# Expert weights in DRAM as pieces of 128 partitions x 4 KB, in a two-layer attention and expert kernel

## The chip, the cores and the metric

The kernel runs on one core of one Trainium2 chip. The metric is the device time of one execution in microseconds (us).

## The reference

The input x has 8 sequences of 100 tokens of width 1024 (800 tokens, float32); each sequence also has a context of 722 rows of width 256. Four blocks follow one another, each as x = x + f(layernorm(x)): cross-attention, a mixture of experts, a second cross-attention, and a feed-forward layer with ternary weights. The change touches the mixture of experts alone:

```
logits = h @ gate_w.T + gate_b                  # 32 experts
topk_logits, topk_idx = top_k(logits, 4);  w = softmax(topk_logits)
gate = h @ w_gate[e] + b_gate[e];  up = h @ w_up[e] + b_up[e]     # 1024 -> 512
act  = (clip(up, -7, 7) + 1) * min(gate, 7) * sigmoid(1.702 * min(gate, 7))
y    = sum over the 4 experts of w * (act @ w_down[e] + b_down[e])  # 512 -> 1024
```

## The kernel before

The expert stage (in the profile from about 1389 to 2240 us) works in blocks of 64 token slots of one expert. 800 tokens x 4 experts, each expert rounded up to whole blocks, are split into three queues of equal length; step s takes block s // 3 of queue s % 3, and each queue has a weight buffer of its own in SBUF (`W2`, NQ_W = 3 buffers of 12,288 floats per partition). The first 8,192 floats of a buffer are the gate and up weights (W2_D = KC x 2 x FI, with KC = 8 chunks of the input width and FI = 512), the other 4,096 the down weights (IC = 4 chunks of D = 1024). In both parts a chunk is 1024 floats, which is 4 KB per partition.

An expert's weights are loaded when its queue reaches it, in order of the first step that needs them: 34 loads, because two experts lie across the border of two queues. Each load is a gate-up DMA of 4 MB (L1372, in the loop L1417), two bias DMAs of 128 KB (L1376, L1420) and a down DMA of 2 MB (L1380, in the loop L1424). All of them are issued by SP, in one queue (q1), in program order. In the loop, SP first waits until the gate-up and bias DMAs of the load before have landed and until TensorE has done the last gate-up that used the buffer; the down DMA waits in the same way for the down DMA before it and for the last down product (L1411 to L1424).

A step on TensorE is: half of the gate-up product (L1518), the transposes of the next tile's tokens (L1510) and of the activations of the step before (L1526), the other half of gate-up, and the down product of the step before (L1542). Gate-up waits for weights and biases (`m_wg`), down for its weights (`m_wd`). VectorE adds the bias (L1607, once a step) and computes the activation together with ScalarE (L1651). ScalarE scales the result by the gate into `ysb` (L1658).

GpSimd moves the tokens on its own DMA queue (q0), in program order: for each pair of steps a gather of 128 rows of 4 KB from `h_d` into `hs` (L1454), for each step a scatter that adds 128 rows of 2 KB to `acc_d` (L1467). It waits for each scatter to land before it starts the next (L1463). ScalarE waits for the scatter before it writes `ysb` again.

In DRAM the weights are `A["W2"]` with shape [32 experts, 128 partitions, 12,288]. So in each partition's row the gate-up part is one run of 32 KB and the down part one run of 16 KB.

Of the kernel before, what the change touches and what calls it, by code (L numbers as in the profile page):

```python
# [16 lines left out]
P = 128  # L17
B, S, D = 8, 100, 1024
L, DC = 722, 256
H, K, DQ, R = 16, 128, 768, 64  # L20
E, TOPK, FI = 32, 4, 512
# [3 lines left out]
TW = [min(P, T - P * m) for m in range(MT)]  # L25
TPAD = MT * P
KC = D // P
# [5 lines left out]
HA = 4  # L33
# [6 lines left out]
IC = FI // P  # L40
# [39 lines left out]
W2_D = KC * 2 * FI  # L80
W2_N = W2_D + IC * D
# [14 lines left out]
C_SPARE = C_HD + 1  # L96
C_FOLD = C_SPARE + 1
C_N = C_FOLD + TW[-1]
assert HA * TW[-1] == P


def constants():
# [59 lines left out]
def build(nc, A, stages=("a0", "moe", "a1", "ffn")):  # L162
    ctx = ExitStack()
    with ctx:
        sems = {}

        def sem(name):
            if name not in sems:
                sems[name] = ctx.enter_context(nc.semaphore(name))
            return sems[name]  # L170
# [82 lines left out]
        W2 = pm.put("W2", [P, NQ_W, W2_N])  # L253
# [121 lines left out]
        def ln_count(p, what, n):  # L375

            each = {"var": 2, "sd": 1, "agg": MT, "hn": MT, "tp": 2 * MT, "ev": 2 * MT}[what]
            return each * ("a0", "moe", "a1", "ffn").index(p) + n
# [990 lines left out]
        def moe_sync(sp):  # L1369

            def load_gate_up(e, q):
                sp.dma_start(W2[:, q, 0:W2_D], A["W2"][e, :, 0:W2_D]).then_inc(sem("m_wg"), 16)  # L1372

            def load_bias(e, q):
                for g in range(G):
                    sp.dma_start(bias3[g * BS:(g + 1) * BS, q, :],  # L1376
                                 A["b2"][e, g:g + 1, :].to_broadcast([BS, N1])).then_inc(sem("m_wg"), 16)

            def load_down(e, q):
                sp.dma_start(W2[:, q, W2_D:W2_N], A["W2"][e, :, W2_D:W2_N]).then_inc(sem("m_wd"), 16)  # L1380

            sp.wait_ge(sem("a_qc"), 16 * HG)
            sp.wait_ge(sem("m_fill"), 16 * HG)
            load_gate_up(0, 0)
            sp.wait_ge(sem("a_folded"), 2)
            sp.dma_start(gwT[:, :, :], A["gwT"].rearrange("p (c e) -> p c e", c=KC)).then_inc(sem("m_gw"), 16)
            sp.dma_start(gb[:, :], A["gb"].to_broadcast([P, E])).then_inc(sem("m_gw"), 16)
            load_bias(0, 0)
            for m in range(MT):
                sp.wait_ge(sem("ln_hn"), ln_count("moe", "hn", m + 1))  # L1390
                sp.dma_start(h_d[m * P:(m + 1) * P, :], HN["moe"][m][:, :]).then_inc(sem("moe_st"), 16)
            sp.wait_ge(sem("m_first"), 1)
            sp.wait_ge(sem("moe_st"), 16 * MT)
            firsts = [0]
            for q in range(1, NQ_W):
                e = sp.value_load(first_e[0:1, q:q + 1], min_val=0, max_val=E - 1)
                sp.wait_ge(sem("m_wg"), GU_INC * q)
                load_gate_up(e, q)
                load_bias(e, q)
                firsts.append(e)  # L1400
            sp.wait_ge(sem("m_tab"), 1)
            for q in range(NQ_W):
                if q == 1:
                    sp.wait_ge(sem("m_gtd"), 16)
                    sp.wait_ge(sem("m_ohg"), 3)
                if q == 2:
                    sp.wait_ge(sem("m_gs"), 2 * G)
                if q:
                    sp.wait_ge(sem("m_wd"), DN_INC * q)
                load_down(firsts[q], q)  # L1410
            with sp.Fori(NQ_W, N_LOADS) as i:  # L1411
                e = sp.value_load(load_i[0:1, 0, bass.ds(i, 1)], min_val=0, max_val=E - 1)
                q = sp.value_load(load_i[0:1, 1, bass.ds(i, 1)], min_val=0, max_val=NQ_W - 1)
                done = sp.value_load(load_i[0:1, 2, bass.ds(i, 1)], min_val=1, max_val=MAX_STEPS)
                sp.wait_ge(sem("m_wg"), GU_INC * i)
                sp.wait_ge(sem("m_gu"), done)
                sp.dma_start(W2[:, bass.ds(q, 1), 0:W2_D].rearrange("p a n -> p (a n)"), A["W2"][e, :, 0:W2_D]).then_inc(sem("m_wg"), 16)  # L1417
                sp.wait_ge(sem("m_act"), done)
                for g in range(G):
                    sp.dma_start(bias3[g * BS:(g + 1) * BS, bass.ds(q, 1), :].rearrange("p a n -> p (a n)"),  # L1420
                                 A["b2"][e, g:g + 1, :].to_broadcast([BS, N1])).then_inc(sem("m_wg"), 16)
                sp.wait_ge(sem("m_wd"), DN_INC * i)
                sp.wait_ge(sem("m_y"), done)
                sp.dma_start(W2[:, bass.ds(q, 1), W2_D:W2_N].rearrange("p a n -> p (a n)"),  # L1424
                             A["W2"][e, :, W2_D:W2_N]).then_inc(sem("m_wd"), 16)
            last = sp.value_load(np_i[0:1, 2:3], min_val=MIN_STEPS - 1, max_val=MAX_STEPS - 1)
            sp.wait_ge(sem("m_gu"), last + 1)
            sp.dma_start(bdt[:, :], A["bd"]).then_inc(sem("m_bt"), 16)
            sp.dma_start(GTt[:, :], gt_d[:, :]).then_inc(sem("m_bt"), 16)
            sp.wait_ge(sem("m_fin"), 1)  # L1430
            for m in range(MT):
                sp.dma_start(yl[m][0:TW[m], :], acc_t[m * P:m * P + TW[m], :]).then_inc(sem(f"m_cg{m // 2}"), 16)
# [556 lines left out]
def layout(i):  # L1989

    def c(a):
        return np.ascontiguousarray(a)

    arr = {"x": c(np.asarray(i["x"]).reshape(T, D)), "ctx": c(np.asarray(i["ctx_512"]))}
    for ly in range(2):
        g = {n: np.asarray(i[f"L{ly}_xattn_{n}"]) for n in ("Wq", "w_kc_q", "w_kc_kv", "W_qr", "W_kr", "Wo")}
        wc = np.zeros((H, P, WC_N), np.float32)
        wc[:, :, WC_R:WC_K] = g["W_qr"].reshape(H, QC, P, R).transpose(0, 2, 1, 3).reshape(H, P, QC * R)
        wkr = g["W_kr"].transpose(0, 2, 1)
        if ly == 0:  # L2000
            arr["WQ0"] = c(g["Wq"].reshape(H, K, KC, P).transpose(0, 3, 2, 1).reshape(H, P, KC * K))
            wc[:, :, WC_C:WC_R] = g["w_kc_q"]
            wc[:, 0:R, WC_K:] = wkr
            wc[:, R:2 * R, WC_K:] = wkr
        else:
            arr["WQ1"] = c(g["Wq"].reshape(H, K, D))
            wc[:, :, WC_C:WC_R] = g["w_kc_q"].reshape(H, K, QC, P).transpose(0, 3, 2, 1).reshape(H, P, DQ)
            wc = c(wc[:, :, 0:WC_K])

            wk = np.zeros((HG, P, HA // 2, DC), np.float32)  # L2010
            for a in range(HA):
                wk[:, (a % 2) * R:(a % 2 + 1) * R, a // 2] = wkr[a::HA]
            arr["WK"] = wk.reshape(HG, P, HA // 2 * DC)
        wb = np.zeros((HG, P, WB_N), np.float32)
        wb[:, :, WB_V:WB_O] = g["w_kc_kv"].reshape(HG, HA, K, CC, P).transpose(0, 4, 1, 3, 2).reshape(HG, P, HA * CC * K)
        wb[:, :, WB_O:] = g["Wo"].reshape(D, HG, HA, K).transpose(1, 3, 2, 0).reshape(HG, P, HA * D)
        arr[f"WC{ly}"], arr[f"WB{ly}"] = wc, wb
    f = {n: np.asarray(i[f"L0_ffn_{n}"]) for n in ("gate_w", "gate_b", "w_gate", "b_gate", "w_up", "b_up", "w_down", "b_down")}
    arr["gwT"] = c(f["gate_w"].reshape(E, KC, P).transpose(2, 1, 0).reshape(P, KC * E))
    arr["gb"] = c(f["gate_b"].reshape(1, E))  # L2020
    arr["bd"] = c(f["b_down"])
    arr["zero"] = np.zeros((1, D), np.float32)
    w2 = np.zeros((E, P, W2_N), np.float32)
    gu = w2[:, :, 0:W2_D].reshape(E, P, KC, G, 2, FH)
    gu[:, :, :, :, 0] = f["w_gate"].reshape(E, KC, P, G, FH).transpose(0, 2, 1, 3, 4)
    gu[:, :, :, :, 1] = f["w_up"].reshape(E, KC, P, G, FH).transpose(0, 2, 1, 3, 4)
    w2[:, :, 0:W2_D] = gu.reshape(E, P, W2_D)
    w2[:, :, W2_D:] = f["w_down"].reshape(E, IC, P, D).transpose(0, 2, 1, 3).reshape(E, P, IC * D)
    arr["W2"] = w2
    arr["b2"] = c(np.concatenate([f["b_gate"].reshape(E, G, FH), f["b_up"].reshape(E, G, FH)], 2))  # L2030
    t = {n: np.asarray(i[f"L1_ffn_W_{n}"]) for n in ("up", "gate", "down")}
    fw = np.zeros((EC, P, 3, D), np.float32)
    for w, n in enumerate(("up", "gate")):
        fw[:, :, w] = t[n].reshape(EC, P, KC, P).transpose(0, 3, 2, 1).reshape(EC, P, D)
    fw[:, :, 2] = t["down"].reshape(D, EC, P).transpose(1, 2, 0)
    arr["F"] = fw.reshape(EC, P, 3 * D)
    arr.update(constants())
    return arr
# [13 lines left out]
```

## Time and profile before

| | |
|---|---|
| median of 3 runs | 3896.39 us (3893.25 to 3897.36) |
| profiled execution, its own time | 3893.81 us |
| its span in the trace | 3892.1 us |
| TensorE (PE) busy | 3594.0 us, 92% of the span |
| VectorE (DVE) busy | 1881.8 us, 48% |
| GpSimd (POOL) busy | 864.1 us, 22% |
| DMA queue q1 (SP): packets, MB, share of 16 engines | 56080, 450.05, 30.3% |
| DMA queue q0 (GpSimd): packets, MB, share | 30880, 93.75, 8.9% |
| expert weights: 34 DMAs of 4096 KB, 34 of 2048 KB | about half of the 450 MB of q1 |

PE is TensorE's matmuls and PEld its weight loads, ACT is ScalarE, SP SyncE, and a q behind an engine's name is its sequencer. An arrow "a <- b" in a wait means that a stood idle until b was done. The share of a DMA queue is the time that its packets took, as a share of the time of all 16 DMA engines. The trace says what the engines did in one execution; releasers of waits are inferred from semaphores.

### The profile page before, as it was taken

The numbers are of one execution on the slowest core, as the hardware profiler recorded it, in microseconds if no ns is written. First come the engines' busy times: TensorE is split into PE (matmuls) and PEld (weight loads), VectorE is DVE, ScalarE is ACT, GpSimd is POOL, SyncE is SP. The second block draws the span as 40 slices with busy tenths as digits, with TensorE's granted clock in tenths as the row PEclk, the third lists the DMA queues.
The fourth block names the chain that finished last, engine by engine and source line by source line (L and its number), as shares of the span: only waits on it lengthen the run. The fifth ranks groups of instructions, "written<-read, shape, count | busy, mean of one in ns | idle before, by whom it ended". The sixth has DMA issues, their size and how long they took to land.

```text
span 3892.1 us, 39006 instructions
## 1 busy us (share of the span) xinstructions
PE 3594.0 (92%) x14156; PEld 1763.2 (45%) x14157; DVE 1881.8 (48%) x1684; ACT 827.8 (21%) x1370; POOL 864.1 (22%) x778
## 2 busy tenths in 40 slices
PE   7899999999999869999999879999999998899999
PEld 4454455445445423333333335445455454554554
DVE  7784475466458441111111137538266285662561
ACT  1220131032022111111111125234143241220110
POOL 5500400310220022212222201000000000891780
PEclk9999999999999979999999989999999999999999
DMA  5621121122112186898779745245143250330320
GB/s 188 224 95 45 61 92 49 59 79 81 46 50 100 42 325 206 288 373 311 255 270 333 272 186 182 78 143 175 71 167 112 95 165 15 131 130 17 129 98 34
DMA packets 90366, 561.50 MB, mean 144 GB/s; under 512 B 10760, under 2 KB 12936, under 8 KB 76320
## 3 DMA queue, kind: packets, MB, share of 16 engines
q1 hardware_dynamic: 56080, 450.05, 30.3%
q0 software_dynamic: 30880, 93.75, 8.9%
q10 hardware_dynamic: 3312, 16.37, 1.2%
q8 instruction: 69, 1.13, 0.1%
q14 instruction: 25, 0.20, 0.0%
HBM read 522.39 MB, written 41.40 MB: 145 GB/s over the span
## 4 chain that ended last, share of the span: by engine, by line
PE 69%; DMA 10%; DVE 9%; issue 5%; POOL 5%; ACT 1%; SPq 1%; POOLq 0%; DVEq 0%; ACTq 0%
PE PS L771 12%; PE PS L757 11%; PE PS L1518 9%; PE PS L885 9%; PE PS L1895 4%; PE PS L1542 4%; DMA bias<-in_b 4%; POOL gtq L1814 4%; PE PS L643 3%; PE PS L658 3%; DVE mx L1056 2%; DMA stg<-in_F 2%; PE PS L875 2%; PE PS L734 2%; PE PS L1868 2%
## 5 line engine op out<-in xcount | busy, mean ns | idle before, releaser
L757 PE MATMUL PS<-qc,kvT 128*128 128x400 f32 x1536 | 544.9, 506 | 8.9 <-DMA kvT<-kvT_d 3.5
L1518 PE MATMUL PS<-W,hT 128*64 128x512 f32 x2208 | 514.4, 609 | 33.3 <-DMA bias<-in_b 32.8
L771 PE MATMUL PS<-Sb,kvN 128*128 128x400 f32 (+1 forms) x1536 | 529.6, 501 | 2.5 <-DVE qc L1072 2.5
L771 PEld LDWEIGHTS PS<-Sb,kvN 128*128 128x128 f32 (+1 forms) x1536 | 293.4, 191 | 231.7 <-issue 11.2
L1116 POOL TENSOR_TENSOR qrope<-rt,rt 128x400 f32<-128x400 f32 x192 | 209.9, 1114 | 827.8 <-DVE rt L1027 827.8
L757 PEld LDWEIGHTS PS<-qc,kvT 128*128 128x128 f32 x1536 | 290.0, 193 | 223.1 <-issue 22.6
L1607 DVE TENSOR_TENSOR gu<-PS,bias 128x512 f32<-128x512 f32 x69 | 47.7, 691 | 679.3 <-PE PS L1518 679.3
L1868 PE MATMUL PS<-xh,wq 128*128 128x400 f16 x2048 | 354.2, 335 | 18.6 <-DVE wq L1744 17.7
L1814 POOL TENSOR_SCALAR gtq<-stg,thr 128x1024 f16<-128x1024 f32 x96 | 311.7, 3259 | 114.6 <-DMA stg<-in_F 114.6
L885 PE MATMUL PS<-wb,ctxl 128*128 128x512 f32 x768 | 331.7, 593 | 4.7 <-ACT ctxl L910 4.7
L1056 DVE TENSOR_REDUCE mx<-Sb 128x400 f32<-128x2400 f32 x64 | 274.3, 4285 | 106.6 <-ACT Sb L991 106.6
L1518 PEld LDWEIGHTS PS<-W,hT 128*64 128x64 f32 x2208 | 155.4, 140 | 331.7 <-issue 300.4
L1868 PEld LDWEIGHTS PS<-xh,wq 128*128 128x128 f16 x2048 | 199.3, 98 | 173.4 <-issue 21.6
L1065 DVE TENSOR_REDUCE sums<-Sb 128x400 f32<-128x2400 f32 x64 | 265.6, 4149 | 0.0
L1027 DVE TENSOR_TENSOR rt<-PS,ropeq 128x800 f32<-128x800 f32 x192 | 180.8, 984 | 164.0 <-PE PS L658 163.9
L1542 PE MATMUL PS<-W,actT 128*64 128x512 f32 x1104 | 250.3, 596 | 2.5 <-ACT actT L1647 2.5
L991 ACT ACTIVATE Sb<-PS 128x400 f32<-128x400 f32 x320 | 159.0, 502 | 414.6 <-PE PS L757 414.6
L1052 DVE TENSOR_TENSOR Sb<-Sb,PS 128x2400 f32<-128x2400 f32 x64 | 169.9, 2654 | 158.3 <-PE PS L859 158.3
L885 PEld LDWEIGHTS PS<-wb,ctxl 128*128 128x128 f32 x768 | 145.3, 190 | 189.7 <-issue 179.9
L1086 DVE TENSOR_TENSOR X<-PS,X 128x512 f32<-128x512 f32 x96 | 66.4, 692 | 305.3 <-PE PS L885 305.3
L1744 DVE SCALAR_TENSOR_TENSOR wq<-stg,nthr,gtq 128x1024 f16<-128x1024 f32 x64 | 141.7, 2253 | 112.2 <-POOL gtq L1814 112.2
L1000 ACT ACTIVATE Sb<-Sb 128x2400 f32<-128x2400 f32 x64 | 141.1, 2205 | 237.4 <-DVE Sb L1052 237.4
(272 smaller groups left out, 3625.9 us busy)
## 6 DMA issues: line engine op xcount, KB each, us to landing
W<-in_W SPq DMA_DIRECT2D x34, 4096.0 KB
W<-in_W SPq DMA_DIRECT2D x34, 2048.0 KB
kvT<-kvT_d SPq DMA_DIRECT2D x64, 768.0 KB, 5.8
kvN<-kvN_d SPq DMA_DIRECT2D x64, 768.0 KB, 4.3
stg<-in_F SPq DMA_DIRECT2D x32, 1536.0 KB, 6.3
absin<-in_F POOLq DMA_DIRECT2D x48, 512.0 KB, 4.2
hn<-in_F POOLq DMA_DIRECT2D x48, 512.0 KB, 3.8
wb<-in_WB SPq DMA_DIRECT2D x8, 2560.0 KB, 9.4
```

The lines of the kernel that those rows point to most:

```text
L757: mm = nc.tensor.matmul(PS[:, lc % 3, 0:GW], kvT[b % 2][:, dc, lc * P:(lc + 1) * P], qc[:, dc, b, :], start=dc == 0, stop=dc == CC - 1)
L771: mm = nc.tensor.matmul(PS[:, 6 + dc, 0:GW], kvN[b % 3][0:k, lc, dc * P:(dc + 1) * P], Sb[b % 3][0:k, lc, :], start=lc == 0, stop=lc == LC ...
L885: mm = nc.tensor.matmul(PS[:, 2 + n % 4, :], ctxl[:, a, m * P:(m + 1) * P], wb[:, w:w + 512], start=a == 0, stop=a == HA - 1)
L1027: ins = nc.vector.tensor_tensor(rt[k % 2][j][:, :, :].rearrange("p i (b s) -> p i b s", b=BH), src, tab, ALU.mult)
L1052: nc.vector.tensor_tensor(sb, sb, PS[:, 4, 0:GW].unsqueeze(1).to_broadcast([P, LC, GW]), ALU.add).then_inc(sem(f"{p}_sb"), 1)
L1056: nc.vector.tensor_reduce(mx[:, :], Sb[st % 3][:, :, :].rearrange("p c n -> p n c"), AX, ALU.max).then_inc(sem(f"{p}_mx"), 1)
L1065: nc.vector.tensor_reduce(sums[:, :], Sb[(st - 1) % 3][:, :, :].rearrange("p c n -> p n c"), AX, ALU.add).then_inc(sem(f"{p}_sum"), 1)
L1116: ins = nc.gpsimd.tensor_tensor(qrope[k % 4][:, i, :], rt[k % 2][0][:, i, :], rt[k % 2][1][:, 1 - i, :], ALU.add)
L1518: mm = nc.tensor.matmul(PS[g * BS:(g + 1) * BS, 2 + u % 2, :], hT2[k][:, c, half * BS:(half + 1) * BS], W2[:, q, o:o + N1], start=c == 0, ...
L1542: mm = nc.tensor.matmul(PS[h * BS:(h + 1) * BS, 4 + u % 2, :], actT[:, j, g * BS:(g + 1) * BS], W2[:, u % NQ_W, o:o + DH], start=c == 0, s ...
L1814: nc.gpsimd.tensor_scalar(gtq[q][:, w, :], stg[q][:, w, :], thr[:, w:w + 1], None, ALU.is_gt).then_inc(sem("f_gt"), 1)
L1868: mm = nc.tensor.matmul(PS[:, 4 * q + 2 * w + half, 0:HALF], wq[q][:, w, c, :], xh[part][:, c, half * HALF:(half + 1) * HALF], start=c == ...
```

## The change

Two things change. In `layout`, the expert weights are stored as [32 experts, 12 chunks, 128 partitions, 1024], so that one chunk of all partitions is a contiguous piece of 512 KB, and within it each partition has 4 KB. In `moe_sync`, the four weight DMAs read their source as 128 partitions x chunks x 1024: 8 pieces per partition for gate-up, 4 for down, 512 KB apart. The buffers in SBUF, the number of DMAs, their bytes, their order and all waits are as before.

```diff
-sp.dma_start(W2[:, q, 0:W2_D], A["W2"][e, :, 0:W2_D]).then_inc(sem("m_wg"), 16)
+sp.dma_start(W2[:, q, 0:W2_D].rearrange("p (c n) -> p c n", c=KC), A["W2"][e, 0:KC].rearrange("c p n -> p c n")).then_inc(sem("m_wg"), 16)
...
-sp.dma_start(W2[:, q, W2_D:W2_N], A["W2"][e, :, W2_D:W2_N]).then_inc(sem("m_wd"), 16)
+sp.dma_start(W2[:, q, W2_D:W2_N].rearrange("p (c n) -> p c n", c=IC), A["W2"][e, KC:KC + IC].rearrange("c p n -> p c n")).then_inc(sem("m_wd"), 16)
...
-sp.dma_start(W2[:, bass.ds(q, 1), 0:W2_D].rearrange("p a n -> p (a n)"), A["W2"][e, :, 0:W2_D]).then_inc(sem("m_wg"), 16)
+sp.dma_start(W2[:, bass.ds(q, 1), 0:W2_D].rearrange("p a (c n) -> p (a c) n", c=KC), A["W2"][e, 0:KC].rearrange("c p n -> p c n")).then_inc(sem("m_wg"), 16)
...
-sp.dma_start(W2[:, bass.ds(q, 1), W2_D:W2_N].rearrange("p a n -> p (a n)"),
-             A["W2"][e, :, W2_D:W2_N]).then_inc(sem("m_wd"), 16)
+sp.dma_start(W2[:, bass.ds(q, 1), W2_D:W2_N].rearrange("p a (c n) -> p (a c) n", c=IC),
+             A["W2"][e, KC:KC + IC].rearrange("c p n -> p c n")).then_inc(sem("m_wd"), 16)
...
-arr["W2"] = w2
+arr["W2"] = c(w2.reshape(E, P, KC + IC, D).transpose(0, 2, 1, 3))
```

## Rows read from the trace of the kernel before

**Rows 1.** The chain that ended last, whole span: shares by engine, by line.
```profile
PE 69%; DMA 10%; DVE 9%; issue 5%; POOL 5%; ACT 1%; SPq 1%; POOLq 0%; DVEq 0%; ACTq 0%
PE PS L771 12%; PE PS L757 11%; PE PS L1518 9%; PE PS L885 9%; PE PS L1895 4%; PE PS L1542 4%; DMA bias<-in_b 4%; POOL gtq L1814 4%; PE PS L643 3%; PE PS L658 3%; DVE mx L1056 2%; DMA stg<-in_F 2%; PE PS L875 2%; PE PS L734 2%; PE PS L1868 2%
```

**Rows 2.** The same chain in order of time, expert stage: start us, us, what.
```profile
1421.29 17.32 DMA bias<-in_b
...
1528.82 3.43 PE PS L1518 x16
...
1533.06 3.58 PE PS L1518 x16
...
1540.08 3.43 PE PS L1518 x16
...
1608.07 17.31 DMA hs<-h_d,idxc
...
1626.38 5.28 PE PS L1518 x16
```

**Rows 3.** Waits in 1380 to 2240 us: total us, times, longest us.
```profile
PE PS L1518 <- DMA bias<-in_b: 32.8, 6, 14.0
...
PE PS L1510 <- DMA hs<-h_d,idxc: 15.6, 4, 8.7
```

**Rows 4.** One line's instructions (L1607), and the landing of another's DMA (scatter L1467).
```profile
L1607 DVE TENSOR_TENSOR gu<-PS,bias x69: 681/692/693, 1402.2 to 2227.7; 128x512 f32<-128x512 f32 x69
...
DMA to landing us min/median/max: 4.5/8.1/17.8
```

**Rows 5.** Timeline of SP and VectorE: start us, us, what.
```profile
8.74 4.27 SPq L444 DMA_DIRECT2D ropek<-in_ropek  x1
...
1604.22 0.69 DVE L1607 TENSOR_TENSOR gu<-PS,bias 128x512 f32<-128x512 f32 x1 [9.12 <-PE PS L1518]
...
1605.96 0.35 SPq L1417 DMA_DIRECT2D W<-in_W  x1
...
1654.43 0.35 SPq L1417 DMA_DIRECT2D W<-in_W  x1
...
1727.74 0.35 SPq L1417 DMA_DIRECT2D W<-in_W  x1
...
1989.15 0.35 SPq L1417 DMA_DIRECT2D W<-in_W  x1
...
2162.86 0.36 SPq L1417 DMA_DIRECT2D W<-in_W  x1
```

**Rows 6.** Packets, MB, engine share in 1236:1241, 4:8, 8:12, 1678:1682 us, in this order.
```profile
q1 hardware_dynamic: 64, 2.10, 97.1%
...
DMA packets 436, 1.60 MB, mean 400 GB/s; under 512 B 45, under 2 KB 45, under 8 KB 436
...
q1 hardware_dynamic: 407, 1.48, 93.7%
...
DMA packets 434, 1.52 MB, mean 379 GB/s; under 512 B 58, under 2 KB 58, under 8 KB 434
...
q1 hardware_dynamic: 219, 0.79, 53.4%
...
q0 software_dynamic: 215, 0.73, 49.7%
...
q1 hardware_dynamic: 48, 1.57, 92.3%
...
q0 software_dynamic: 48, 0.10, 13.2%
```

**Rows 7.** GpSimd's queue q0 in 2020:2170 us, then 1654:1746 us.
```profile
q0 software_dynamic: 2766, 6.80, 20.0%
...
q0 software_dynamic: 1338, 3.29, 14.2%
```

**Rows 8.** Busy time of each engine, granted clock, DMA share, GB/s in run B.
```profile
1654.00:1746.00 92.00, 84.44 (x398) 29.25 (x395) 16.55 (x40) 14.32 (x30) 16.31 (x25) 0.98 0.98 379
```

More of the change, by code:

```diff
@@ L98 @@
 C_N = C_FOLD + TW[-1]
-assert HA * TW[-1] == P
+assert HA * TW[-1] == P and 2 * FI == D
 def constants():
```

## The prediction

> **What bounds the kernel now.** I read the chain that ended last first, for the whole span: TensorE holds 69% of it and DMA 10%, and among the DMA pieces the largest are those of the bias loads [rows 1]. Then the same chain inside the expert stage, which is the only stage that the change touches. There it alternates between two things [rows 2]: pieces of L1518 and L1542 in the fixed pattern 3.43, 3.58, 3.43 us, one expert block each 11.26 us (1528.82 to 1540.08), and DMA pieces of 16 to 18 us each. A bias load is only 128 KB; its 17.32 us is the 4 MB weight load in front of it in the same queue, so "DMA bias" reads as "expert weights have landed". The waits of the stage say what this costs [rows 3]: TensorE stood 32.8 us for weights (6 times) and 15.6 us for gathered tokens (4 times). Behind each stall of 2.4 us or more the first half block runs slow: 5.28 us at 1626.38 against 3.58 us at other places [rows 2]. The 69 bias additions L1607 start from 1402.2 to 2227.7 [rows 4]: 825.5 us for 68 steps that at 11.26 us would be 765.7. So about 60 us of 3893.8 is all that this stage has to give; the rest is TensorE at its pace.
>
> Which load serves which block I worked out from the reference's router: it fills 67 blocks of 64 (two spare ones make three queues of 23), and the 34 loads serve steps 0, 1, 2, 3, 5, 6, 7, 14, 16, 17, 19, 23, 24, 25, 27, 28, 31, 34, 36, 37, 38, 43, 45, 48, 49, 51, 55, 57, 59, 61, 63, 64, 66, 67. Experts of one block crowd together, and there SP issues a load each time the last has landed: the runs A (steps 1 to 7, until about 1493), S (16, 17), B (23 to 28), C (36 to 38), D (48, 49) and E (63 to 67). The issue times show it [rows 5]: in B 73.3 us from 1654.43 to 1727.74 for four loads, 18.3 us each, in A, C, S, D and E 16 to 20 us apart.
>
> **How the DMA engines serve it.** I then looked at packets. While the 4 MB load runs alone, 64 packets of 32 KB move in 5 us at a 97.1% share: 5 x 16 x 0.971 / 64 = 1.214 us each [rows 6]. When x is loaded in rows of 4 KB, 407 packets, 361 of them rows by the bytes and the others the small ones that end a DMA, take 4 x 16 x 0.937 = 60.0 us: 0.166 us a row, the small ones included [rows 6]. And while a scatter runs beside a weight load, the two queues get 48 packets each in 4 us [rows 6]: they take turns packet by packet, 2 KB against 32 KB, so each of the 8 packets that an engine moves for a scatter waits a 32 KB one, 1.33 us a pair. That is why a gather takes 17.31 us there [rows 2], and why scatters take up to 17.8 us with a median of 8.1 and a least of 4.5 [rows 4]. GpSimd does all of them in order, one scatter a block, so at 17 us each it falls behind blocks of 11.26 us, and the gather for a later tile is late: the hs pieces of the chain [rows 2].
>
> **The change, part by part.**
> - Weight loads. The bytes, the number of DMAs and their order stay. Each 32 KB row becomes 8 pieces of 4 KB at a distance of 512 KB in DRAM, each 16 KB row 4 pieces. A turn (one gate-up, one down, two bias loads) is now 8 x 1.214 + 8 x 0.607 = 14.6 us of weights per engine; it becomes 96 pieces. A piece costs between 1.214 / 8 = 0.152 us (nothing lost) and 0.173 us (the 379 GB/s of 4 KB rows beside another queue: 4096 x 16 / 379e9 [rows 6]). I take 0.159, between 0.152 and the 0.166 that carries one small packet in nine: 15.3 us, so +0.7 us a turn; the ends give 0 and +2.0.
> - SP. One DMA now carries 1,024 pieces. Issuing is 0.35 us now; nothing in the trace has so many pieces. Some of the issues may block on a full queue, as ropek's did for 4.27 us with 15 loads ahead [rows 5]; SP then waits with 5 us or more of work queued, which delays nothing. Cost 0; if it left DMA empty for 1 us a load, 20 us over the runs.
> - Gathers and scatters. They now wait for a 4 KB piece: 8 pairs of about 0.33 us instead of 1.33, so some 8 us less, 16 to 17 becoming about 8. That is under 11.26 us, GpSimd keeps up, and the token stalls go: 15.6 us, three slow restarts of 5.28 - 3.58 = 1.7 us, and one block 1.3 us late on a scatter: gain 22 us.
> - What they now take from the weights. DMA does the same total, but gathers and scatters that were held back inside a run are now served inside it, and the last weights of the run land that much later. In an undelayed stretch 2766 of their packets pass in 150 us, 18.4 per us at 0.174 us each (20.0% x 16 x 150 / 2766) [rows 7]. In B it was 1338, where TensorE's 84.44 us of work would make 1557: 219 missing, 14 per engine, 2.3 us [rows 7, 8]. The same way: A 2.5 us, S 1.5, C 0.7, D 2.7, E 0.8 until its second load and 1.1 to its end.
>
> Per run, turns x 0.7 plus this, less the slack that the run has before TensorE needs the weights (gate-up of a step starts 3.43 us after the L1607 before it). A: 6 turns, 4.2 + 2.5 = 6.7. B: 5 turns, 3.5 + 2.3 = 5.8. C: 3 turns, 2.1 + 0.7 = 2.8. S: 1.4 + 1.5, slack 1607.65 - 1605.96 = 1.7: 1.2. D: 1.4 + 2.7, slack 1990.6 - 1989.15 = 1.5: 2.6, and a restart 1.7. E: its second load 1.4 + 0.8 less 2163.6 - 2162.86 = 0.7: 1.5; its last lands some 3.9 later than about 2197.5, needed at 2197.4 plus 1.5: 2.5 and a restart 1.7 [rows 2, 5]. Together 26.5 us lost against 22 gained: +4.5. The other stages have no edit. The profiled execution took 3893.8, 2.6 below the median, so the forecast is 3893.8 + 4.5 + 2.6 = 3901.
>
> **The rivals.** *Small packets are free.* If a piece costs 0.152 us, only the displaced packets are left: A 2.5, B 2.3, C 0.7, D 1.2, E about 1, S 0: 7.7 against 22, so 14 us faster, 3882; if TensorE does not even feel those, 3874. For it: 0.166 carries small packets, and the overlap at shares above 100% hides some of the gap. Against it: 419 GB/s in the one row and 400 in the other [rows 6].
>
> *The jumps cost.* The other sign by one mechanism: each engine now hops 512 KB from piece to piece, which no load of the trace does. Over 22 turns, 0.173 us a piece gives 1.3 x 22 = 29 us more, 3929. It decides early: 0.15 us a turn more, a piece of 0.161 us, and the kernel is slower by over 0.2%. For it: 379 GB/s is the 4 KB rate when queues mix. Against it: rows of 4 KB otherwise hold 400.
> The Trainium skill (DMA: Bandwidth & Descriptors, Latency and other measured facts) has copies at 207 GB/s with a pitch of 512 KB between partitions against 214 with a padded one. Taken over as an estimate, 3.4% of a turn is 0.5 us, and the sum would come to about 3912; here the pitch lies between pieces of one partition, and no row shows it.
>
> *The unit of turns stays large.* If the pieces of one load are served several at a time before the other queue gets its turn, the gathers wait as now, the token stalls stay, and only the piece price is paid where runs bind: 6 + 5 + 3 turns x 0.7 and 0.7 in E, 3896.4 + 10.5 = 3907. Against it: rows of 4 KB and another queue's packets shared 4 us as 219 to 215 [rows 6].
> The Trainium skill (DMA: Bandwidth & Descriptors, Queues, rings and completion order) says that an engine drains a whole packet of typically 9 to 17 descriptors before it changes rings; by that this rival would hold, while the counts here are one for one.
>
> **How the numbers follow.** Of this kernel 0.2% is 7.8 us, about what a measurement can tell from no change. Forecast (3889 to 3904): 0.42. Small packets free: 0.24. Jumps cost, or SP's issue does: 0.24. Unit stays large: 0.10. Faster 0.24, same 0.42, slower 0.34. The range takes in the two bounds of the piece price, 3876 to 3929; I leave what lies outside to chance. The predicted time is the forecast's own, 3901; its own range is 3889 to 3904.
>
> **What the profile after would show.** Weight packets of 4 KB, some 52,000 of them, at a mean near 0.16 us; scatter landings with a median near 5 to 6 us and a largest near 8 instead of 17.8; no wait of TensorE for hs, and more than 32.8 us of waits for bias; L1417 issues in B about 18 to 19 us apart. I am wrong if the spacing in B grows beyond 19.5 us (jumps), shrinks (free packets), or the scatters stay at 16 us (unit).

## The result

| | kernel before | changed kernel |
|---|---|---|
| median | 3890.19 us (3882.8 to 3900.05, 20 runs) | 3902.32 us (3896.54 to 3909.06, 20 runs) |
| ratio | | 1.0032, 95% interval 1.0026 to 1.0039 |
| profiled execution | 3893.81 us | 3899.25 us |
| expert stage in the trace | 838.3 us | 847.1 us |

The change makes the kernel slower by 0.32%, 12 us. The forecast was 4.5 us slower, inside the 0.2% (7.8 us) that I called no change. The time, 3902.32, lies in the stated range of 3889 to 3904 and 1.3 us from the forecast of 3901. Read as a difference it does not: the range lay around a time before of 3896.39, the median of 3 runs, so it allowed 7.6 us slower, and 12 were measured. By "expert stage" I mean from here on the stretch from the issue of the first down load (L1380) to the last bias addition (L1607). It is the better measure for single profiles: over the twelve profiles of this case the rest of the kernel, which no edit touches, took 3049 to 3058 us, while the stage of two executions of one kernel agreed within 1.4 us.

The page of the changed kernel: the span, the packets in all, the two queues, and the chain by engine and by line.

```profile
span 3897.5 us, 39006 instructions
...
DMA packets 133886, 561.50 MB, mean 144 GB/s; under 512 B 10760, under 2 KB 12936, under 8 KB 128544
...
q1 hardware_dynamic: 99600, 450.05, 31.3%
q0 software_dynamic: 30880, 93.75, 8.7%
...
PE 67%; DMA 11%; DVE 9%; POOL 6%; issue 5%; SPq 1%; ACT 1%; DVEq 0%; ACTq 0%; POOLq 0%
PE PS L771 12%; PE PS L757 11%; PE PS L885 9%; PE PS L1518 8%; DMA bias<-in_b 7%; PE PS L1895 4%; POOL gtq L1814 4%; PE PS L1542 4%; PE PS L643 3%; PE PS L658 3%; DVE mx L1056 2%; DMA stg<-in_F 2%; PE PS L875 2%; PE PS L734 2%; PE PS L670 1%
```

The same bytes now move in 43,520 more packets: 34 x 128 x 12 of 4 KB in the place of 34 x 128 x 2. The bias loads, which stand for "expert weights have landed", rose from 4% of the chain to 7% [rows 1]. The waits of the stage (total us, times, longest us):

```profile
POOL sidxc L1463 <- DMA acc_d<-ysb,sidxc: 336.5, 68, 7.8
...
PE PS L1518 <- DMA bias<-in_b: 55.4, 13, 18.2
```

TensorE waits 55.4 us for weights instead of 32.8, and the waits for gathered tokens (15.6 us before [rows 3]) are not there any more: 7.0 us of waits more in all, of the 8.9 by which the stage grew. GpSimd stood 336.5 us for its scatters; before it was 453.6, with 15.8 us the longest. The additions L1607 and the landing of the scatters (L1467) answer to [rows 4]:

```profile
L1607 DVE TENSOR_TENSOR gu<-PS,bias x69: 683/692/693, 1399.2 to 2233.5; 128x512 f32<-128x512 f32 x69
...
DMA to landing us min/median/max: 4.6/8.2/9.4
```

No scatter takes more than 9.4 us where the largest was 17.8; the 68 steps take 834.3 us instead of 825.5. The timeline of SP (start us, us, what) shows the weight loads of run B, and the bias issue that stood longest:

```profile
1386.43 0.40 SPq L1380 DMA_DIRECT2D W<-in_W  x1
...
1418.17 4.79 SPq L1420 DMA_DIRECT2D bias<-in_b  x2
...
1657.17 0.39 SPq L1417 DMA_DIRECT2D W<-in_W  x1
...
1733.63 0.39 SPq L1417 DMA_DIRECT2D W<-in_W  x1
```

In B four loads take 76.5 us, 19.1 each, instead of 73.3 and 18.3 [rows 5]. And the packets while the first gate-up load runs alone (1233 to 1238 us: packets, MB, share of 16 engines):

```profile
q1 hardware_dynamic: 500, 2.05, 100.9%
```

5 x 16 x 1.009 / 500 = 0.161 us each, where a 32 KB packet took 1.214 [rows 6], or 0.152 for each 4 KB of it. With 96 pieces that is 15.5 us a turn instead of 14.6: +0.9.

From the starts of the 69 additions in both traces, the delay of each block above 11.26 us, summed by run:

| run | lost, forecast | lost, measured | gained, measured |
|---|---|---|---|
| A (steps 1 to 7) | 6.7 | 9.3 | |
| S (16 to 19) | 1.2 | 1.5 | 5.0 (step 18) |
| B (23 to 28) | 5.8 | 6.8 | 1.3 (step 26) |
| C (36 to 38) | 2.8 | 2.2 | |
| D (48 to 50) | 4.3 | 0.4 | 4.2 (step 50) |
| E (63 to 67) | 5.7 | 10.5 | 11.2 (step 66) |
| sum | 26.5 | 30.7 | 21.7 (forecast 22) |

Net 8.9 us, which is what the stage grew by. The medians differ by 12.1 with an interval of 10 to 15; the profile of before was taken of an execution 3.6 us above its median, that of after of one 3.1 below, and the rest of the kernel (3053.9 and 3050.4 us in them) accounts for the difference. With the second profiles of both kernels, below, the stage grew by 8.9 to 11.0 us; what remains of 1 to 3 us between it and the medians I can't place.

### The profile page after: what moved, and what is told of

It reads as the page before. It is cut to its first block, busy times and chain, and to the rows that moved or that the text cites. A ratio compares the mean times of both kernels' runs of the same rounds, so it can differ in the third digit from the quotient of the medians.

```text
span 3897.5 us, 39006 instructions
## 1 busy us (share of the span) xinstructions
PE 3592.5 (92%) x14156; PEld 1761.1 (45%) x14157; DVE 1880.9 (48%) x1684; ACT 828.1 (21%) x1370; POOL 863.5 (22%) x778
## 4 chain that ended last, share of the span: by engine, by line
PE 67%; DMA 11%; DVE 9%; POOL 6%; issue 5%; SPq 1%; ACT 1%; DVEq 0%; ACTq 0%; POOLq 0%
PE PS L771 12%; PE PS L757 11%; PE PS L885 9%; PE PS L1518 8%; DMA bias<-in_b 7%; PE PS L1895 4%; POOL gtq L1814 4%; PE PS L1542 4%; PE PS L643 3%; PE PS L658 3%; DVE mx L1056 2%; DMA stg<-in_F 2%; PE PS L875 2%; PE PS L734 2%; PE PS L670 1%
## 5 line engine op out<-in xcount | busy, mean ns | idle before, releaser
L1518 PE MATMUL PS<-W,hT 128*64 128x512 f32 x2208 | 516.4, 611 | 55.4 <-DMA bias<-in_b 55.4
L1607 DVE TENSOR_TENSOR gu<-PS,bias 128x512 f32<-128x512 f32 x69 | 47.7, 692 | 689.1 <-PE PS L1518 689.1
## 6 DMA issues: line engine op xcount, KB each, us to landing
W<-in_W SPq DMA_DIRECT2D x34, 2048.0 KB, 10.8
```

The lines of the kernel that those rows point to most:

```text
L1518: mm = nc.tensor.matmul(PS[g * BS:(g + 1) * BS, 2 + u % 2, :], hT2[k][:, c, half * BS:(half + 1) * BS], W2[:, q, o:o + N1], start=c == 0, ...
```

## The experiments

The theory: the turns of the runs that bind grew because a 4 KB packet costs more per byte ("piece price"), and the token waits went because gathers and scatters wait for short packets. The rivals: the hop of 512 KB costs ("jumps"), or the loss is the traffic of GpSimd that is now served inside the runs ("displacement"). Ratios are against the kernel before on the same chip (its medians were 3889 to 3891 us). Each "expected" text below was written before its run; e3, e4 and e9 are one edit with three piece sizes.

| run | pieces | median us | ratio, 95% interval | stage us | waits for weights, tokens |
|---|---|---|---|---|---|
| before, two profiles | 32 and 16 KB | 3890.19 | | 838.3, 836.9 | 32.8, 15.6; 28.7, 18.3 |
| changed, first result | 4 KB, 512 KB apart | 3902.32 | 1.0032, 1.0026 to 1.0039 | 847.1 | 55.4, none |
| e1 changed again | the same | 3903.22 | 1.0031, 1.0019 to 1.0043 | 847.9 | 58.3, none |
| e2 | 4 KB, in one row | 3900.63 | 1.0026, 1.0015 to 1.0036 | 847.6 | 55.9, none |
| e9 | 2 KB, 256 KB apart | 3927.08 | 1.0094, 1.0080 to 1.0108 | 868.2 | 75.1, none |
| e3 | 8 KB, 1 MB apart | 3887.07 | 0.9990, 0.9981 to 0.9998 | 833.6 | 46.2, none |
| e4 | 16 KB, 2 MB apart | 3879.41 | 0.9974, 0.9964 to 0.9985 | 826.4 | 34.9, 3.3 |
| e10 | 16 KB, in one row | 3879.93 | 0.9974, 0.9963 to 0.9985 | 824.0 | 38.9, none |
| e5, no scatters | as before | 3865.87 | 0.9935, 0.9922 to 0.9948 | 808.8 | 25.7, none |
| e6, no scatters | as changed | 3874.90 | 0.9959, 0.9945 to 0.9972 | 819.5 | 34.7, none |
| e7, no scatters | 16 KB | 3867.98 | 0.9939, 0.9927 to 0.9951 | 810.0 | 24.6, 2.1 |

### e1: the changed kernel again

> The changed kernel once more, on the chip of the next three. It is slower by 0.2 to 0.4% (8 to 15 us) if the first result holds. Its profile shows how far single executions differ: the waits of TensorE for weights should be near 55 us, those for gathered tokens none.

As expected in ratio, waits and stage; in the last run of the stage step 64 lost 1.6 us instead of 4.2. So single blocks differ by a few us between executions, and the stage by 0.8.

### e2: pieces of 4 KB in one row of DRAM

Against the changed kernel; of each line only the part that differs:

```diff
-A["W2"][e, 0:KC].rearrange("c p n -> p c n")
+A["W2"][e, :, 0:KC, 0:D]
...
-arr["W2"] = c(w2.reshape(E, P, KC + IC, D).transpose(0, 2, 1, 3))
+arr["W2"] = np.zeros((E, P, KC + IC, D + 64), np.float32)
+arr["W2"][:, :, :, 0:D] = w2.reshape(E, P, KC + IC, D)
```

> Pieces of 4 KB as in the change, but all 12 of a partition lie in one row of DRAM, 4352 bytes apart instead of 512 KB. Theory 'piece price' (a 4 KB packet costs more per byte than one of 16 or 32 KB, wherever it lies): as the changed kernel, ratio 1.002 to 1.004, TensorE waits near 55 us for weights. Rival 'jumps' (the hop of 512 KB costs): most of the loss goes, ratio 0.998 to 1.000, spacing of loads in run B back to 18.3 us from 19.1.

The loss stays: 1.0026, and the stage is 847.6 us against 847.1 and 847.9. The waits of TensorE and the packets of the first load alone (1232 to 1237 us):

```profile
PE PS L1518 <- DMA bias<-in_b: 55.9, 12, 18.5
...
q1 hardware_dynamic: 512, 2.10, 102.5%
```

0.160 us a packet, 12 waits of 55.9 us, and in run B the loads stay 19.2 us apart: the profile can't be told from that of the changed kernel. The jumps cost nothing that these runs can see, and that rival falls. The Trainium skill (DMA: Bandwidth & Descriptors, Latency and other measured facts) has 3% less for copies with a pitch of 512 KB between partitions; for 512 KB between the pieces of one partition no run here shows it (1.0031 against 1.0026, intervals overlapping).

### e3, e4, e10: pieces of 8 and 16 KB

Shown for 16 KB, against the changed kernel and only the parts that differ; 8 KB has PW = 2048 (and the 2 KB of e9 PW = 512), and each expression that named KC, IC or D in the four loads and in the layout now names GP, DP or PW. e10 places the 16 KB pieces in one row as e2 does its own, with 64 floats between them.

```diff
+PW = 4096
+GP, DP = W2_D // PW, IC * D // PW
...
-c=KC), A["W2"][e, 0:KC]
+c=GP), A["W2"][e, 0:GP]
...
-w2.reshape(E, P, KC + IC, D).transpose(0, 2, 1, 3)
+w2.reshape(E, P, GP + DP, PW).transpose(0, 2, 1, 3)
```

> Pieces of 8 KB: 4 for a gate-up load and 2 for a down load, 1 MB apart. Piece price: half the packets, so half of what 4 KB pieces cost above 32 KB ones; scatters wait about 0.48 us a pair and land within about 10 us, under a block's 11.26, so the token waits stay gone (gain 22 us) and the losses fall from 30 to about 20 us: ratio 0.998 to 1.001. Rival 'displacement' (the loss is the gathers and scatters served inside the runs, whatever the packets): ratio as the changed kernel, 1.002 to 1.003. Rival 'jumps': with half as many hops, between the two.

> Pieces of 16 KB: 2 for a gate-up load, 1 for a down load, 2 MB apart. Piece price: none left. A pair is 0.61 + 0.18 us, so a scatter in a run lands after about 4.6 + 7 = 11 to 12 us, at the edge of a block's 11.26: GpSimd falls behind slowly, most token waits go, and less is displaced in the runs. Ratio 0.996 to 0.999, faster than before. If displacement alone sets the loss: 0.999 to 1.001, with token waits under 5 us.

> Pieces of 16 KB that lie in one row of DRAM, 16,640 bytes apart instead of 2 MB. If the size of the packets alone decides, it equals the kernel with 16 KB pieces 2 MB apart, ratio 0.996 to 0.998, the stage 826 us within 2. If the place in DRAM matters, it differs from that by over 0.1%.

16 KB pieces are faster than both kernels, by 0.26% against before. 8 KB pieces are faster than before by 0.10%, with an interval that ends at 0.9998. All three ratios lie where the piece price was expected to put them, and below what displacement alone would give (1.002 to 1.003 for 8 KB, 0.999 to 1.001 for 16 KB). In run B the loads are 18.3 us apart with 16 KB pieces and 18.4 with 8 KB ones, against 18.3 before and 19.1 with 4 KB. Only the gate-up load differs between 16 KB pieces and the kernel before, whose down load has runs of 16 KB anyway: two packets per partition in the place of one. The waits and the scatter's landing with 16 KB pieces:

```profile
PE PS L1520 <- DMA bias<-in_b: 34.9, 8, 8.1
...
PE PS L1512 <- DMA hs<-h_d,idxc: 3.3, 1, 3.3
...
DMA to landing us min/median/max: 4.3/9.5/13.4
```

The largest landing is 13.4 us instead of 17.8, more than the 11 to 12 expected and above a block's 11.26, and one token wait of 3.3 us is left. Two stretches of it: the first load alone (1231 to 1236 us), and a scatter beside a weight load (1672 to 1676 us).

```profile
q1 hardware_dynamic: 136, 2.23, 103.9%
...
q1 hardware_dynamic: 89, 1.46, 85.7%
q0 software_dynamic: 91, 0.25, 19.7%
```

5 x 16 x 1.039 / 136 = 0.611 us a packet, half of a 32 KB one, so no price; and 89 packets to 91: still one for one, with each weight packet half as long. The same in the changed kernel, from 1690 to 1692 us:

```profile
q1 hardware_dynamic: 102, 0.42, 54.9%
q0 software_dynamic: 98, 0.19, 51.3%
```

With 8 KB pieces the largest landing is 10.8 us and no token wait is left, and 5 x 16 x 1.019 / 263 = 0.310 us a packet makes 14.9 us a turn:

```profile
q1 hardware_dynamic: 263, 2.15, 101.9%
...
DMA to landing us min/median/max: 4.5/9.2/10.8
...
PE PS L1520 <- DMA bias<-in_b: 46.2, 11, 14.3
```

The 16 KB pieces in one row give 0.9974 again. The stage is 2.4 us shorter, a little more than the 2 us expected, with no difference in the median: the place in DRAM does not matter here either.

### e5, e6, e7: without the scatters

In each, GpSimd only counts `m_sc` up in the place of the scatter; the experts' results are left out of the output.

```diff
-nc.gpsimd.indirect_dma_start(out=acc_d[:, :], ..., in_=ysb[k][:, :], in_offset=None, compute_op=ALU.add).then_inc(sem("m_sc"), 16)
+pool.sem_inc(sem("m_sc"), 16)
```

> The kernel before without its 69 scatters: GpSimd only signals where it scattered, so the experts' results are left out of the output; gathers, weights and products stay. The token waits should go (15.6 us and their restarts, 22 us in all), and the runs lose the scatters' share of DMA, some 1.6 us of each turn: 25 to 40 us faster than before, ratio 0.990 to 0.994. It is the base for the next two, in which hardly anything is left that could be displaced.

> The changed kernel without its scatters, the same part left out. Theory 'piece price': against the kernel before without scatters it loses 0.7 to 0.9 us for each of the 14 turns of runs A, B and C that bind, 8 to 13 us, and nothing is gained, since no token waits are left there. Rival 'displacement': the two without scatters are equal within 3 us.

> Pieces of 16 KB without scatters, the same part left out. By both theories it equals the kernel before without scatters within 3 us: 16 KB packets cost no more than 32 KB ones, and what 16 KB pieces gained was the token waits, which are gone in both. If it is faster than that base by more, 16 KB packets are better for another reason.

Without its scatters the kernel before is 24.7 us faster, a ratio of 0.9935, 0.3 us less than the 25 to 40 expected, and its token waits are gone. The waits of TensorE for weights, e5:

```profile
PE PS L1517 <- DMA bias<-in_b: 25.7, 4, 12.3
```

and e6:

```profile
PE PS L1517 <- DMA bias<-in_b: 34.7, 7, 14.1
```

With next to nothing to displace and no token wait to win, 4 KB pieces still cost 10.7 us of stage (819.5 - 808.8) and 9.0 in the medians, inside the 8 to 13 that the piece price gives for the 14 turns of A, B and C. The theory of displacement, which said equal within 3 us, falls as the main cause. 16 KB pieces without scatters are within 1.2 us of stage and 2.1 of the median from e5, so their gain in the whole kernel comes from the token waits, as far as 2 us can be told.

### e8: the kernel before again

> The kernel before once more, for a second profile of it: 825 us from the first to the last bias addition within 2 us, and the waits for weights and tokens at the same blocks as in the first profile (3, 7, 25, 38 and 18, 50, 66).

The distance from the first to the last addition was 820.0 us, not 825 within 2: step 3 lost 10.4 us instead of 16.0, because the first addition itself came 16.9 us after the first down load's issue instead of 12.8. The stage as defined above was 836.9 us. The token waits stood at the same blocks, 18, 50 and 66 (18.3 us in all, with two more of a fraction). This is why the stage is counted from the first down load's issue.

### e9: pieces of 2 KB

> Pieces of 2 KB, half of the change's. The bias loads' packets of 2 KB take 0.084 us at the least; 192 of them are 16.1 us a turn against 96 x 0.1615 = 15.5 with 4 KB and 14.6 with 16 and 32 KB. Piece price: 0.6 us more than the changed kernel in each of 22 turns, the stage 10 to 16 us longer than the changed kernel's 847, ratio to before 1.005 to 1.008. Displacement: the gathers and scatters are served at once with 4 KB already, so no more is displaced, and the time equals the changed kernel's, 1.002 to 1.004.

The time rose further, as only the piece price says: 1.0094, above the 1.005 to 1.008 expected, and the stage is 21 us above the changed kernel's, more than the 10 to 16. The waits, the landing of the scatters, and the first load alone (1233 to 1238 us):

```profile
PE PS L1520 <- DMA bias<-in_b: 75.1, 13, 19.4
...
DMA to landing us min/median/max: 4.6/7.9/9.1
...
q1 hardware_dynamic: 867, 1.78, 96.5%
```

0.089 us a packet, not the 0.084 that I had taken from the bias loads: 17.1 us a turn, +1.6 over 4 KB, of which run B shows 1.07 (20.2 us between loads instead of 19.1). 22 turns of 1.07 make 24 us, near the 21 that the stage grew by; at 1.6 it would be 35. The times of the packets overlap: over run B they add up to 102% of the engines' time here, and to 98% in the changed kernel. The scatters land hardly sooner than with 4 KB (9.1 us at most instead of 9.4).

## Why the prediction was right in kind and too small in size

- **What bounds the stage** held. Losses and gains fell on the runs that were named, and run B's spacing grew from 18.3 to 19.1 us, at the upper end of the 18 to 19 forecast. The restart after a stall, 5.28 us instead of 3.58, is TensorE's clock: after the wait for tokens it was granted 0.50 from 1626.5 to 1629.9 us (the 1.2 GHz level) and 1.00 behind that, and 3.4 us at half speed are the 1.7 us.
- **The absolute time was hit in part by luck.** Of two errors one hid the other: the change cost 7.6 us more than forecast (12.1 instead of 4.5), and the time before, taken from 3 runs, was 6.2 us too high (3896.39, where 20 runs have 3890.19). The outcome that I gave the most, no change at 0.42, did not come; "slower", at 0.34, did.
- **Token waits gone, gain 22 us**: measured 21.7 us by step, and no wait for hs in the profile. The mechanism is shown by the series of largest landings, 17.8, 13.4, 10.8 and 9.4 us for packets of 32, 16, 8 and 4 KB. My guess of 5 to 6 us for the median was too low: it was 8.2, after 8.1. A scatter beside which q1 moves next to nothing lands after 4.5 to 5.1 us in both kernels; beside weights the median fell from 11.0 to 8.6 us, but more scatters now run beside weights (q1 moved over 0.2 MB a us beside 53 of the 69, before beside 46). By the forecast's pairs it would be about 6 there (my estimate, 4.7 + 8 x 0.161); what makes it 8.6 no run shows.
- **The weight piece, +0.7 us a turn**, is the term that was too small. I took 0.159 us a piece, where it measured 0.161, so +0.9 a turn. Over the 22 turns that is 4 to 5 us, as much as lies between the forecast's 4.5 and the measured 8.9 us of stage; but only run B fits by itself (5 turns, 1.0 more than forecast). A lost 2.6 more, C 0.6 less, D 3.9 less and E 4.8 more, so the rest is slack and traffic that happen to cancel. I had written myself that 0.161 is where the kernel becomes slower by over 0.2%, and then chose a value 1% below a bound that decided the sign. e2, e6 and e9 show that the piece's size, and nothing about where it lies, makes this price: 10.7 us without scatters, and 20.7 us between 16 and 4 KB pieces with them (847.1 - 826.4), 0.94 for each of the 22 turns.
- **Displacement**, forecast at 7.7 us behind the slack of the runs (the rival of free packets has it alone), was about right, though not the main cause (e6). Pieces of 16 KB cost nothing by themselves and win 21.7 less one wait of 3.3 and its restart of 0.7, about 18; their stage is shorter by 11.9, so some 6 us are lost to the traffic that is now served inside the runs. In e10, with no token wait, it is 21.7 less 14.3, 7.4 us. These are differences of stages, not a run of their own. For run B the forecast of 219 packets more was too high: 1440 with 16 KB pieces against 1338 and 1396 in the two profiles of before.
- **The slack in D and E** was off both ways: D lost 0.4 us where 4.3 was forecast, E 10.5 where it was 5.7. Both hang on whether a load lands within 1 to 3 us of its need. e1 has 0.7 and 8.6 there, so the split between the steps is partly chance.
- **SP's issues** did block as supposed: the bias issues behind a gate-up load of 1,024 pieces stood for 2 to 5 us in eleven places. In all eleven the 16 DMA engines were 98 to 108% busy, so I leave it at no cost; no run tried it alone. With pieces of 2 KB, SP stood 7 to 10 us behind the loads of the runs.
- **The rivals.** "Jumps cost" fell (e2, e10). "Unit stays large" fell: 102 packets to 98 with 4 KB pieces, and landings that shrink with the packet. "Small packets are free" fell; at 16 KB it would have been right. The rule of the Trainium skill (DMA: Bandwidth & Descriptors, Queues, rings and completion order) that an engine drains some 9 to 17 descriptors before it changes rings does not hold for these transfers, where the queues take turns after each run of up to 32 KB.

## What to carry to other kernels

Where two DMA queues share the engines, they take turns packet by packet, and a packet is a contiguous run of up to 32 KB: long runs in one queue lengthen every small gather or scatter in the other (up to 17.8 us where 4.7 is usual alone). Cutting the runs buys that latency back, but only until the small DMA fits into its slot of the loop; past that, each halving only adds the packets' fixed cost to a transfer that may itself be the bound. Cut to the longest run that still lets the small DMA keep pace, here 16 KB, which all but does (13.4 us at most for a slot of 11.26), and when a term's two bounds lie on both sides of the sign, say so in the chances instead of taking the middle.

## What the runs showed that I had not expected

The time of a packet, with a load running alone: 1.214 us for 32 KB, 0.611 for 16, 0.310 for 8, 0.161 for 4 and 0.089 for 2 KB. Per 32 KB that is 1.21, 1.22, 1.24, 1.29 and 1.42 us, so the price is small down to 8 KB and grows fast below. The first 4 MB load as a whole, from its first packet to its last, says the same over the twelve profiles: 10.2 to 10.4 us with 32 KB, 10.3 to 10.5 with 16, 10.4 with 8, 10.7 to 11.2 with 4 and 12.2 with 2 KB. Even 8 KB is not free where turns bind: 0.3 us a turn over 32 KB, and e3's stage is 7.2 us longer than e4's. And a place 512 KB or 2 MB away for the next piece costs no more that these runs can tell than one just behind (1.0031 against 1.0026, 0.9974 against 0.9974).
